# Feed-forward stage of a decoder layer: merged operations on pairs, norms ahead of expert products, and the leftover weight summed on ScalarE

## The chip, the cores and the metric

The kernel runs on one core of one Trainium2 chip. The metric is device time in microseconds of one launch. TensorE (PE) multiplies matrices, VectorE (DVE) and ScalarE (ACT) work on rows of 128 partitions, GpSimd (POOL) does the same work more slowly, and SyncE (SP) issues transfers. Each engine takes its own instructions strictly in the order in which the program lists them; engines meet only at semaphores.

## The reference

The layer has three parts, each added to the residual: a bidirectional minGRU, a cross-attention over a context of 1601 rows, and a product-key feed-forward with 256 experts. The change touches only the last part:

```python
q = (hidden_states @ Wq + bq).reshape(B, S, H, QD)          # 2048 tokens, 8 heads of 64
q = (q - mean) / jnp.sqrt(var + EPS_BN) * bn_gamma + bn_beta
q0, q1 = _l2norm(q[..., :HALF]), _l2norm(q[..., HALF:])
s0 = jnp.einsum('bshq,kq->bshk', q0, k0)                    # 32 keys each
s1 = jnp.einsum('bshq,kq->bshk', q1, k1)
ts0, ti0 = jax.lax.top_k(s0, DTK)                           # the 4 best of 32, twice
...
w = jax.nn.softmax(top_s, axis=-1)                          # over the 16 pairs
eh = gelu(einsum('bshkd,bsd->bshk', expert_down[idx], hidden_states))
out = jnp.einsum('bshko,bshk->bso', expert_up[idx], eh * w)
```

The kernel never gathers. It forms, for each token and head, a dense row of 256 weights as an outer product of 8 first-key and 32 second-key factors, sums the heads, multiplies by the gelu of all 256 expert products, and multiplies by `expert_up`.

## The kernel before

Only `stage_ffn` is touched. 2048 tokens make 16 tiles of 128 (`TILES`), two tiles make a group (`PER`), so there are 8 groups. The queries lie transposed in `raw` and `qT`, in four chunks of 128 features (`QC`), so that a group is 4 chunks of 256 columns.

Preparation. `normed` applies the batch norm (scale and bias) to the queries chunk by chunk: DVE for groups 0 and 1 (L1415), POOL for 2 and 3 (L1197), ACT from 4 on (L1274). `squared` squares them into `sq` (L1281 on ACT, L1190 and L1193 on POOL). On PE `norms(n)` (L1614) sums squares by head with 16 small products, `scores(i)` (L1625) makes a tile's scores, and `expert_product(m)` (L1602), eight in all, makes 512 tokens by 128 experts into one of four banks, which ACT's `gelu(m)` empties (L1257). Banks 0 and 1 of them are later those of `sum_heads`, banks 2 and 3 those of `mix`.

The loop over tiles i, as each engine lists it:
- DVE (L1542): `scaled(i+1)` multiplies scores by the inverse norms; `largest(i, 1)` finds the 8 largest of each head's second half, and between its instructions it issues `weight_steps` of the group before (at even i): sums, reciprocals, `share`, `first` (the 8 first-key factors), then the reduction `own` (L1507) and `clamped` = 8 - own (L1511), which releases POOL by `weights_ready`. Then at some even i `squares(k)` waits for a batch of norms; then `weigh(i-4)` (L1529) waits for `sum_heads(i-4)`; then `largest(i, 0)` and `remove(i)`, which releases POOL's `selected(i)`.
- ACT (L1322): `exponentials(i+1)` waits for `scaled(i+1)`; at even i perhaps `norm_roots`; at i = 2 the gelus 4 to 7; at odd i `normed(n+3)` and `squared(n+3)`; then `read_output(i-5)`. Sqrt, Exp and Gelu lie in different tables, and a change of table is an instruction of its own.
- POOL (L1229): `selected` (writes `near`) and two `products` per tile, each an outer product over four heads (L1152). After the first one POOL adds `clamped` to a single column of `prod` (L1218), and this lets `sum_heads` go.
- PE (L1699): `scores(i+2)`, at even i `norms(n+2)`, `mix(i-5)` (L1650), `sum_heads(i-3)` (L1634), which needs both products.

`prod` has three buffers. The last two tiles, and half of tile 13, are shared between POOL and DVE (`SHARE`).

Of the kernel before, what the change touches and what calls it, by code (L numbers as in the profile page):

```python
# [11 lines left out]
P = 128  # L12
# [999 lines left out]
def stage_ffn(nc, keep, d):  # L1012
# [27 lines left out]
    with ExitStack() as ctx:  # L1040
# [27 lines left out]
        share = st.sb("share", [P, PER * HEADS, FIRSTS])  # L1068
# [15 lines left out]
        def query(c, a, e):  # L1084
            return raw[:, c, a:e] if a < SEQ else qT[:, c, a - SEQ:e - SEQ]

        def expert_bank(m):
# [17 lines left out]
        weights_ready, prod_ready, prod_done, part_pool, part_dve, weight_mm, h_ready, out_mm = (  # L1105
            st.sem(n) for n in ("weights_ready", "prod_ready", "prod_done", "part_pool", "part_dve", "weight_mm",
# [17 lines left out]
        def wait_squares(eng, n, c):  # L1124

            if n == 0 and c < ACT_CHUNKS:
                eng.wait_ge(sq_ready, c + 1)
            elif n < 2:
                eng.wait_ge(sq_pool, QC * n + c + 1 - ACT_CHUNKS)
            else:  # L1130
                eng.wait_ge(sq_ready, ACT_CHUNKS + QC * (n - 2) + c + 1)

        def wait_query(eng, n, chunks):

            if n < FIRST_POOL:
                eng.wait_ge(q_ready_dve, QC * n + chunks)
            elif n < FIRST_ACT:
                eng.wait_ge(q_ready_pool, QC * (n - FIRST_POOL) + chunks)
            else:
                eng.wait_ge(q_ready_act, QC * (n - FIRST_ACT) + chunks)  # L1140
# [16 lines left out]
        with nc.Block() as block:  # L1157
# [11 lines left out]
            def _(pool):  # L1169
# [4 lines left out]
                pool.tensor_tensor(kinv[:], k2[:], mhalf[:], ALU.pow).then_inc(kinv_ready, 1)  # L1174
                pool.memset(pair[:], 0.0).then_inc(pair_ready, 1)
# [5 lines left out]
                pool.wait_ge(const_ready, 1)  # L1181
# [4 lines left out]
                pool.wait_ge(const_ready, 5)  # L1186
# [3 lines left out]
                for c in range(ACT_CHUNKS, QC):  # L1190
                    pool.wait_ge(q_ready_dve, c - ACT_CHUNKS + 1)
                    pool.tensor_tensor(sq[:, 0, c], q0[:, c], q0[:, c], ALU.mult).then_inc(sq_pool, 1)
                for c in range(QC):  # L1193
                    pool.wait_ge(q_ready_dve, QC + QC)
                    q = query(c, COLS, 2 * COLS)
                    pool.tensor_tensor(sq[:, 1, c], q, q, ALU.mult).then_inc(sq_pool, 1)
                for n in range(FIRST_POOL, FIRST_ACT):  # L1197
                    for c in range(QC):
                        q = query(c, n * COLS, (n + 1) * COLS)
                        pool.tensor_scalar(q, q, bn[:, 0:1], bn[:, 1:2], ALU.mult, ALU.add).then_inc(q_ready_pool, 1)  # L1200
# [42 lines left out]
            def _(act):  # L1243
# [30 lines left out]
                def normed(n):  # L1274

                    for c in range(QC):
                        q = query(c, n * COLS, (n + 1) * COLS)
                        act.activation(q, q, ACT.Identity, scale=bn[:, 0:1], bias=bn[:, 1:2])\
                            .then_inc(q_ready_act, 1)

                def squared(n):  # L1281
                    if n >= 2:
                        act.wait_ge(norm_mm, n - 1)
                    else:
                        act.wait_ge(bn_ready, 1)
                    for c in range(QC if n else ACT_CHUNKS):
                        q = query(c, n * COLS, (n + 1) * COLS)
                        if n >= 1:
                            wait_query(act, n, c + 1)
                            act.activation(sq[:, n % 2, c], q, ACT.Square).then_inc(sq_ready, 1)  # L1290
                        else:
                            act.activation(sq[:, 0, c], q, ACT.Square, scale=bn[:, 0:1], bias=bn[:, 1:2])\
                                .then_inc(sq_ready, 1)
# [28 lines left out]
                for i in range(TILES):  # L1322
# [10 lines left out]
                    if t == 1 and n + 3 < GROUPS:  # L1333
                        if n + 3 >= FIRST_ACT:
                            normed(n + 3)
                        squared(n + 3)
                    if i - WEIGH - 1 >= 0:
                        read_output(i - WEIGH - 1)
                read_output(ADDED - 1)

            @block.vector
            def _(dve):
# [72 lines left out]
                def normed():  # L1415

                    for c in (*range(ACT_CHUNKS, QC), *range(ACT_CHUNKS)):
                        dve.tensor_scalar(q0[:, c], query(c, 0, COLS), bn[:, 0:1], bn[:, 1:2], ALU.mult, ALU.add)\
                            .then_inc(q_ready_dve, 1)
                    for c in range(QC):  # L1420
                        q = query(c, COLS, 2 * COLS)
                        dve.tensor_scalar(q, q, bn[:, 0:1], bn[:, 1:2], ALU.mult, ALU.add).then_inc(q_ready_dve, 1)
# [61 lines left out]
                def weight_steps(n, a=0, e=PER):  # L1484
                    h = n % 2
                    part = [P, (e - a) * HEADS, FIRSTS]
                    lists = top[:, h, a:e].rearrange("p t h k -> p (t h) k")[:, :, 0:2 * TOPK].rearrange(
                        "p h (s k) -> p h s k", s=2)
                    kept = near[:, h, a:e].rearrange("p t h k -> p (t h) k")
                    rows = slice(a * HEADS, e * HEADS)  # L1490
                    c = note(dve.tensor_reduce(total[:, rows], lists, AX.X, ALU.add))
# [6 lines left out]
                    c = note(dve.tensor_tensor(share[:, rows], kept[:, :, 0:FIRSTS], inv[:, rows, 1:2].broadcast_to(part),  # L1498
# [3 lines left out]
                    c = note(dve.tensor_tensor(first[:, h, a:e].rearrange("p t h i -> p (t h) i"), share[:, rows],  # L1502
                                               inv[:, rows, 0:1].broadcast_to(part), ALU.mult))
                    if n * PER + e > LASTS - 1:
                        need(c)
                        dve.tensor_copy(lead[:, a:e], first[:, h, a:e])
                    c = note(dve.tensor_reduce(own[:, a:e], share[:, rows].rearrange("p (t h) i -> p t (h i)", t=e - a),  # L1507
                                               AX.X, ALU.add))
                    yield
                    need(c)  # L1510
                    dve.tensor_scalar(clamped[:, h, a:e], own[:, a:e], -1.0, float(HEADS), ALU.mult, ALU.add)\  # L1511
                        .then_inc(weights_ready, 1)
                    yield
# [77 lines left out]
            def _(pe):  # L1591
# [33 lines left out]
                def scores(i):  # L1625
                    wait_query(pe, i // PER, QC)
# [7 lines left out]
                def sum_heads(i):  # L1634
# [3 lines left out]
                    if i < LASTS:  # L1638
                        pe.wait_ge(prod_done, 2 * (i + 1) - (i in SHARE))
# [10 lines left out]
                def mix(i):  # L1650
                    if i >= 2:
                        wait_output(pe, i - 2)
                    if i < ADDED:
# [31 lines left out]
                pe.wait_ge(const_ready, 5)  # L1685
# [5 lines left out]
                expert_product(4)  # L1691
# [3 lines left out]
                for m in range(EARLY_GELU + 1, ES):  # L1695
                    expert_product(m)
# [85 lines left out]
```

## Time and profile before

| | before |
|---|---|
| median of 3 runs | 433.55 us (432.21 to 433.97) |
| the profiled execution, its own time | 433.55 us |
| its span, first to last instruction | 431.8 us |
| around the span | 1.75 us |
| PE busy | 402.8 us, 93% |
| DVE busy | 307.4 us, 71% |
| ACT busy | 225.7 us, 52% |
| POOL busy | 207.7 us, 48% |
| mean granted clock of TensorE | 0.980 |

The shares are means over three unlike parts. The feed-forward runs from 306 us on, its preparation ends about 352 us and the loop over tiles fills the rest. Matmuls are pipelined, and so a row that stands for several of them is a little longer than the distance to the next row.

### The profile page before, as it was taken

To read this page: it belongs to the slowest core of one execution; us is meant where nothing else is said; L and a number is where in the kernel's file an instruction comes from. 1 tells how busy PE (TensorE), PEld (TensorE's weight loads), DVE (VectorE), ACT (ScalarE), POOL (GpSimd) and SP (SyncE) were. 2 spreads that over 40 slices of the span, in tenths; PEclk is the share of its full clock that TensorE was granted. 3 is DMA by queue.
4 is the path that set the end of the run, shared out by engine and by line. 5 is a ranking of instruction groups with operands and counts; after the bars stand their busy time and mean duration, and the time that the engine had idled before them with its cause. 6 is when DMAs were issued, how large, how long until landed. Compare 5 with 4: busy or idle time off the path is not lost. (4 is left out here: it accounts for less than half of the span.)

```text
span 431.8 us, 7774 instructions
## 1 busy us (share of the span) xinstructions
PE 402.8 (93%) x2563; PEld 368.9 (85%) x2563; DVE 307.4 (71%) x1139; ACT 225.7 (52%) x455; POOL 207.7 (48%) x203
## 2 busy tenths in 40 slices
PE   2997999987999999999999999999999979999786
PEld 2876878876899999999999999989778979999685
DVE  5899885667656575476755555565876889899995
ACT  3774646314645455555554444444557878675300
POOL 2588988941814233342333312000112668899991
PEclk9999999999999999999999999999999877999989
DMA  7800222002322223211232100000000000001011
GB/s 227 275 2 3 74 71 77 8 0 77 102 76 77 52 77 99 56 50 53 76 93 61 53 2 2 1 2 1 26 0 2 1 2 2 27 26 37 27 35 52
DMA packets 19992, 21.38 MB, mean 50 GB/s; under 512 B 3180, under 2 KB 16624, under 8 KB 19952
## 3 DMA queue, kind: packets, MB, share of 16 engines
q1 hardware_dynamic: 18832, 19.96, 15.5%
q10 hardware_dynamic: 1120, 0.92, 0.8%
q8 instruction: 21, 0.34, 0.3%
q14 instruction: 19, 0.16, 0.1%
HBM read 18.78 MB, written 2.10 MB: 48 GB/s over the span
## 5 line engine op out<-in xcount | busy, mean ns | idle before, releaser
L960 PE MATMUL att_pA<-context_cNh,att_pTh 128*128 128x256 f32 (+1 forms) x208 | 62.6, 301 | 1.1 <-DVE att_pTl L858 1.1
L961 PE MATMUL att_pA<-context_cNl,att_pTh 128*128 128x256 f32 (+1 forms) x208 | 58.3, 280 | 0.0
L962 PE MATMUL att_pA<-context_cNh,att_pTl 128*128 128x256 f32 (+1 forms) x208 | 58.1, 280 | 0.0
L1152 POOL TENSOR_TENSOR ffn_prod<-ffn_first,ffn_near 128x1024 f32<-128x1024 f32 (+1 forms) x29 | 54.6, 1882 | 7.0 <-DVE ffn_clamped L1511 6.6
L858 DVE TENSOR_TENSOR att_pTl<-att_pR,att_pTh 128x512 fp32r<-128x512 f32 x64 | 37.4, 586 | 26.7 <-ACT att_pTh L775 26.5
L877 DVE TENSOR_REDUCE att_mx<-keep_pQ 128x1 f32<-128x402 f32 x64 | 35.6, 568 | 25.5 <-PE keep_pQ L77 25.4
L765 POOL TENSOR_TENSOR context_cTl<-keep_raw,context_cTh 128x512 fp32r<-128x512 f32 (+1 forms) x24 | 23.1, 978 | 47.9 <-ACT context_cTh L789 47.9
L765 POOL TENSOR_TENSOR context_cNl<-keep_raw,context_cNh 128x512 fp32r<-128x512 f32 (+1 forms) x21 | 25.1, 1210 | 41.9 <-ACT context_cNh L789 41.9
L960 PEld LDWEIGHTS att_pA<-context_cNh,att_pTh 128*128 128x128 f32 (+1 forms) x208 | 39.1, 188 | 2.2 <-DVE att_pTl L858 1.5
L1646 PE MATMUL ffn_pT<-keep_ident,ffn_prod 128*128 128x128 f32 x256 | 34.7, 294 | 6.5 <-POOL ffn_prod L1152 3.9
L1646 PEld LDWEIGHTS ffn_pT<-keep_ident,ffn_prod 128*128 128x128 f32 x256 | 32.0, 153 | 9.4 <-DVE ffn_hT L1533 4.7
L961 PEld LDWEIGHTS att_pA<-context_cNl,att_pTh 128*128 128x128 f32 (+1 forms) x208 | 39.3, 189 | 0.0
L962 PEld LDWEIGHTS att_pA<-context_cNh,att_pTl 128*128 128x128 f32 (+1 forms) x208 | 39.1, 188 | 0.0
L775 ACT ACTIVATE att_pTh<-att_pR 128x512 fp32r<-128x512 f32 x64 | 32.4, 516 | 9.3 <-PE att_pR L992 8.5
L219 POOL TENSOR_TENSOR gru_z<-gru_z,gru_g 128x512 f32<-128x512 f32 x16 | 31.2, 1950 | 8.3 <-DVE gru_g L407 8.3
L992 PE MATMUL att_pR<-keep_ident,att_prob 128*128 128x128 f32 (+1 forms) x208 | 32.8, 272 | 0.0
L1467 DVE MAX8 ffn_top<-ffn_e 128x8 f32<-128x32 f32 x256 | 29.5, 176 | 0.3
L75 PE MATMUL gru_pP<-gru_xTh,gru_wh 128*128 128x512 f32 x62 | 26.9, 434 | 0.0
L775 ACT ACTIVATE att_vTh<-att_pR 128x256 fp32r<-128x256 f32 x16 | 6.1, 384 | 39.4 <-PE att_pR L997 39.4
L75 PE MATMUL keep_pQ<-context_cTh,keep_qT0h 128*128 128x402 f32 (+1 forms) x64 | 23.0, 359 | 3.2 <-PEq L159 1.7
L379 DVE TENSOR_TENSOR_SCAN gru_hT<-gru_c,gru_z 128x512 f32<-128x512 f32 x16 | 24.1, 1508 | 2.2 <-POOL gru_z L219 1.6
L992 PEld LDWEIGHTS att_pR<-keep_ident,att_prob 128*128 128x128 f32 (+1 forms) x208 | 24.8, 140 | 0.7
(285 smaller groups left out, 1138.7 us busy)
## 6 DMA issues: line engine op xcount, KB each, us to landing
keep_raw<-in_ctxT SPq DMA_DIRECT2D x24, 256.0 KB, 2.6
keep_raw<-in_ctx SPq DMA_DIRECT2D x24, 256.0 KB, 2.7
out<-keep_x SPq DMA_DIRECT2D x16, 128.0 KB, 1.7
keep_x<-in_x SPq DMA_DIRECT2D x3, 512.0 KB, 10.0
gru_wout<-in_W_out SPq DMA_DIRECT2D x1, 512.0 KB, 8.4
keep_raw<-in_fWq SPq DMA_DIRECT2D x2, 256.0 KB
keep_raw<-in_ctxT SPq DMA_DIRECT2D x8, 32.5 KB, 3.6
keep_raw<-in_ctx SPq DMA_DIRECT2D x4, 65.0 KB
```

What stands on the lines that cost most here:

```text
L75: pe.matmul(out, lh, rh, start=(i == 0), stop=False)
L219: pool.tensor_tensor(z[:, n % ZB], z[:, n % ZB], g[:, u % 2], ALU.mult).then_inc(zg_ready, 1)
L765: pool.tensor_tensor(lo, raw(i % RAW), hi.bitcast(F32), ALU.subtract).then_inc(piece_lo, 1)
L775: act.activation(to, bank, ACT.Copy).then_inc(bank_high, 1)
L858: dve.tensor_tensor(to, bank, half(it, 0, n)[0].bitcast(F32), ALU.subtract).then_inc(bank_free, 1)
L877: last = dve.tensor_reduce(mx[:, h, j:j + 1], pS[:, j, 0:min(SPANS[j][1], CTX) - SPANS[j][0]], AX.X, ALU.max)
L960: pe.matmul(pA[:, 0:D], l[0], r[0], start=(kt == 0), stop=False)
L961: pe.matmul(pA[:, 0:D], l[0], r[1], start=False, stop=False)
L962: last = pe.matmul(pA[:, 0:D], l[1], r[0], start=False, stop=(kt == CT - 1))
L992: last = pe.transpose(bank[0:rows, m * P:(m + 1) * P], prob[:, a % 2, kt * P:kt * P + rows], ident[:])
L1152: return eng.tensor_tensor(prod[:, i % PB, a:b].rearrange("p h (i j) -> p h i j", j=KEYS), (factor if factor is not None else first[:, n % ...
L1646: last = pe.matmul(pW[:, i % 2, c * P:(c + 1) * P], prod[:, i % PB, h, c * P:(c + 1) * P], ident[:], start=(h == 0), stop=(h == HEADS - 1) ...
```

## The change

Six edits, all in `stage_ffn`:
1. `normed` and `squared` take a whole group in one instruction (128x1024), or a pair of chunks (128x512) for group 0 and for POOL's squares. Their semaphores count groups.
2. On PE `norms(1)` moves ahead of expert product 4 and `norms(2)` ahead of product 5; `norms(3)` goes ahead of `scores(4)`; products 6 and 7 move into the loop, behind `scores(5)` at i = 3.
3. The first `sum_heads` waits for six gelus where it waited for eight; the first `mix` waits for eight.
4. DVE's `own` and `clamped` and POOL's addition go, for tiles 0 to 13. In their place ACT gets `leftover(i)`: a Copy with scale -1 over 65 numbers, with its sum taken (64 shares and a constant -8), then an addition of the sum to the one column of `prod`. For the last group DVE keeps its own way.
5. `weights_ready` is set by `first`. `sum_heads(i)` waits for `last_ready` of ACT and for the second product.
6. `leftover(i-3)` stands in ACT's loop at i, behind `exponentials(i+1)`, `normed` and `squared`.

```diff
-                        pool.wait_ge(prod_ready, i + 1)
-                        last = prod[:, i % PB, 0, EXPERTS - 1:EXPERTS]
-                        pool.tensor_tensor(last, last, clamped[:, n % 2, t:t + 1], ALU.add).then_inc(prod_done, 1)
...
-                    for c in range(QC):
-                        q = query(c, n * COLS, (n + 1) * COLS)
-                        act.activation(q, q, ACT.Identity, scale=bn[:, 0:1], bias=bn[:, 1:2])\
-                            .then_inc(q_ready_act, 1)
+                    act.activation(queries(n), queries(n), ACT.Identity, scale=bn[:, 0:1], bias=bn[:, 1:2])\
+                        .then_inc(q_ready_act, 1)
...
+                        wait_query(act, n)
+                        act.activation(sq[:, n % 2], queries(n), ACT.Square).then_inc(sq_ready, 1)
...
+                def leftover(i):
+
+                    n, t = i // PER, i % PER
+                    act.wait_ge(weights_ready, weights_at(i))
+                    act.wait_ge(const_ready, 6)
+                    rest = clamped[:, n % 2, t:t + 1]
+                    act.activation(spare[:], share[:, n % 2, t], ACT.Copy, scale=-1.0, accum_out=rest).then_inc(own_ready, 1)
+                    act.wait_ge(prod_ready, i + 1)
+                    act.wait_ge(own_ready, i + 1)
+                    last = prod[:, i % PB, 0, EXPERTS - 1:EXPERTS]
+                    act.activation(last, last, ACT.Identity, bias=rest).then_inc(last_ready, 1)
...
                         if n + 3 >= FIRST_ACT:
                             normed(n + 3)
                         squared(n + 3)
+                    if i >= SUM:
+                        leftover(i - SUM)
                     if i - WEIGH - 1 >= 0:
                         read_output(i - WEIGH - 1)
+                leftover(LASTS - 1)
                 read_output(ADDED - 1)
...
                     if i < LASTS:
-                        pe.wait_ge(prod_done, 2 * (i + 1) - (i in SHARE))
+                        pe.wait_ge(last_ready, i + 1)
+                        if i not in SHARE:
+                            pe.wait_ge(prod_done, i + 1)
...
-                expert_product(4)
                 norms(1)
                 scores(2)
                 scores(3)
-                for m in range(EARLY_GELU + 1, ES):
-                    expert_product(m)
+                expert_product(EARLY_GELU)
                 norms(2)
+                expert_product(EARLY_GELU + 1)
                 pe.wait_ge(ld_up, 16)
                 for i in range(TILES):
                     n, t = i // PER, i % PER
+                    if i == PER:
+                        norms(n + 2)
                     if 4 <= i + 2 < TILES:
                         scores(i + 2)
+                    if i == PER + 1:
+                        for m in range(EARLY_GELU + 2, ES):
+                            expert_product(m)
...
                         if i == SUM:
-                            pe.wait_ge(gelu_ready, ES)
+                            pe.wait_ge(gelu_ready, EARLY_GELU + 2)
                         sum_heads(i - SUM)
```

## Rows read from the trace of the kernel before

**Rows 1.** Busy time in stretches: us, PE, PEld, DVE, ACT, POOL, granted clock, DMA.
```profile
350.00:360.00 10.00, 7.18 (x45) 6.72 (x44) 9.02 (x69) 9.13 (x20) 5.43 (x6) 0.66 0.01 2
360.00:370.00 10.00, 10.00 (x72) 9.80 (x72) 8.68 (x74) 7.51 (x20) 9.65 (x9) 0.83 0.05 14
370.00:380.00 10.00, 10.00 (x81) 9.54 (x80) 8.69 (x72) 6.69 (x17) 7.85 (x9) 1.00 0.04 14
```

**Rows 2.** The chain in order of time, one turn of PE's loop: start, us, what.
```profile
368.62 0.89 PE keep_pQ L1631 x8
369.52 1.68 PE ffn_pK L1622 x16
371.20 0.54 PE keep_pQ L1654 x2
...
372.60 1.75 PE ffn_pT L1646 x16
```

**Rows 3.** Timeline of POOL: start, us, line, operation, tiles, [idle before <-releaser].
```profile
372.13 1.91 POOL L1152 TENSOR_TENSOR ffn_prod<-ffn_first,ffn_near 128x1024 f32<-128x1024 f32 x1 [2.00 <-DVE ffn_clamped L1511]
...
386.76 1.91 POOL L1152 TENSOR_TENSOR ffn_prod<-ffn_first,ffn_near 128x1024 f32<-128x1024 f32 x1
388.75 0.19 POOL L1218 TENSOR_TENSOR ffn_prod<-ffn_prod,ffn_clamped 128x1 f32<-128x1 f32 x1
388.89 0.86 POOL L1205 TENSOR_TENSOR ffn_near<-ffn_e,ffn_picked 128x320 f32<-128x320 f32 x1
```

**Rows 4.** Timeline of ACT between i = 2 and i = 4.
```profile
353.45 1.09 ACT L1260 ACTIVATE ffn_gT<-keep_pQ 128x512 f32<-128x512 f32 x2
354.56 1.28 ACT L1305 ACT_TABLE_LOAD   x1
355.85 0.42 ACT L1305 ACTIVATE ffn_e<-ffn_s 128x256 f32<-128x256 f32 x1
...
356.79 2.06 ACT L1278 ACTIVATE ffn_qT<-ffn_qT,ffn_bn 128x256 f32<-128x256 f32 x4
358.76 1.32 ACT L1290 ACTIVATE ffn_sq<-ffn_qT 128x256 f32<-128x256 f32 x4
```

**Rows 5.** Timeline of PE where the preparation ends and summing begins.
```profile
350.47 1.60 PE L1631 MATMUL keep_pQ<-ffn_keyT,ffn_qT 128*128 128x128 f32 x8
354.60 3.51 PE L1646 MATMUL ffn_pT<-keep_ident,ffn_prod 128*128 128x128 f32 x16 [2.52 <-ACT ffn_gT L1260]
```

**Rows 6.** Timeline of DVE: `weigh(0)`, `scaled(6)`, `squares(3)`, `scaled(8)`, `squares(4)`, the tail's first product.
```profile
359.69 0.41 DVE L1533 TENSOR_TENSOR ffn_hT<-ffn_pT,ffn_gT 128x256 f32<-128x256 f32 x1
...
362.32 0.68 DVE L1459 TENSOR_TENSOR ffn_s<-keep_pQ,ffn_ninv 128x512 f32<-128x512 f32 x1
...
371.24 0.23 DVE L1429 TENSOR_SCALAR ffn_n<-ffn_pK 128x64 f32<-128x64 f32 x1 [1.58 <-PE ffn_pK L1622]
...
374.81 0.68 DVE L1459 TENSOR_TENSOR ffn_s<-keep_pQ,ffn_ninv 128x512 f32<-128x512 f32 x1
...
390.85 0.21 DVE L1429 TENSOR_SCALAR ffn_n<-ffn_pK 128x64 f32<-128x64 f32 x1
...
416.75 1.21 DVE L1152 TENSOR_TENSOR ffn_prod<-ffn_pB,ffn_near 128x1024 f32<-128x1024 f32 x1
```

**Rows 7.** Groups of ACT by form: tiles, count | busy us, mean ns | idle before.
```profile
L810 ACT ACTIVATE att_prob<-keep_pQ,att_nmax 128x1206 f32<-128x1206 f32 x16 | 20.3, 1270 | 5.7 <-DVE att_nmax L884 4.4
...
L1278 ACT ACTIVATE ffn_qT<-ffn_qT,ffn_bn 128x256 f32<-128x256 f32 x16 | 8.2, 586 | 0.0
L1290 ACT ACTIVATE ffn_sq<-ffn_qT 128x256 f32<-128x256 f32 x24 | 7.9, 401 | 0.0
...
L813 ACT ACTIVATION_READ_ACCUMULATOR att_prob<-keep_pQ,att_nmax 128x1 f32 x16 | 3.2, 200 | 0.0
...
L1298 ACT ACTIVATE ffn_nroot<-ffn_n 128x32 f32<-128x32 f32 x2 | 0.5, 230 | 1.1 <-DVE ffn_n L1429 1.1
```

**Rows 8.** The two groups of DVE that go, by form.
```profile
L1507 DVE TENSOR_REDUCE ffn_own<-ffn_share 128x2 f32<-128x128 f32 x6 | 1.7, 277 | 0.0
...
L1511 DVE TENSOR_SCALAR ffn_clamped<-ffn_own 128x2 f32<-128x2 f32 x6 | 1.2, 194 | 0.0
```

More of the change, by code:

```diff
@@ L1085, in query, with queries @@
             return raw[:, c, a:e] if a < SEQ else qT[:, c, a - SEQ:e - SEQ]
+        def queries(n, a=0, e=QC):
+            lo, hi = n * COLS, (n + 1) * COLS
+            return raw[:, a:e, lo:hi] if lo < SEQ else qT[:, a:e, lo - SEQ:hi - SEQ]
         def expert_bank(m):
@@ L1283, in squared @@
                         act.wait_ge(norm_mm, n - 1)
+                        wait_query(act, n)
+                        act.activation(sq[:, n % 2], queries(n), ACT.Square).then_inc(sq_ready, 1)
                     else:
                         act.wait_ge(bn_ready, 1)
[L1286 to L1293, printed above, removed]
+                        act.activation(sq[:, 0, 0:ACT_CHUNKS], queries(0, 0, ACT_CHUNKS), ACT.Square, scale=bn[:, 0:1],
+                                       bias=bn[:, 1:2]).then_inc(sq_ready, 1)
                 def norm_roots(k):
@@ L1415, in normed @@
                 def normed():
[L1417 to L1422, printed above, removed]
+                    for c in (ACT_CHUNKS, 0):
+                        dve.tensor_scalar(q0[:, c:c + ACT_CHUNKS], queries(0, c, c + ACT_CHUNKS), bn[:, 0:1], bn[:, 1:2],
+                                          ALU.mult, ALU.add).then_inc(q_ready_dve, 1)
+                    dve.tensor_scalar(queries(1), queries(1), bn[:, 0:1], bn[:, 1:2], ALU.mult, ALU.add)\
+                        .then_inc(q_ready_dve, 1)
                 def squares(k):
@@ L1497, in weight_steps @@
                     dve.wait_ge(near_ready, n * PER + e)
-                    c = note(dve.tensor_tensor(share[:, rows], kept[:, :, 0:FIRSTS], inv[:, rows, 1:2].broadcast_to(part),
+                    if n >= 2:
+                        dve.wait_ge(own_ready, (n - 1) * PER)
+                    c = note(dve.tensor_tensor(shares, near[:, h, a:e, :, 0:FIRSTS], by[:, :, :, 1:2].broadcast_to(part),
                                                ALU.mult))
@@ L1501, in weight_steps @@
                     need(c)
-                    c = note(dve.tensor_tensor(first[:, h, a:e].rearrange("p t h i -> p (t h) i"), share[:, rows],
-                                               inv[:, rows, 0:1].broadcast_to(part), ALU.mult))
-                    if n * PER + e > LASTS - 1:
+                    scaled_shares = dve.tensor_tensor(first[:, h, a:e], shares, by[:, :, :, 0:1].broadcast_to(part), ALU.mult)
+                    if n < GROUPS - 1:
+                        scaled_shares.then_inc(weights_ready, 1)
+                        if n * PER + e == LASTS:
+                            dve.wait_ge(weights_ready, weights_at(LASTS - 1))
+                            dve.tensor_copy(lead[:, a:e], first[:, h, a:e])
+                        yield
+                    else:
+                        c = note(scaled_shares)
                         need(c)
                         dve.tensor_copy(lead[:, a:e], first[:, h, a:e])
[L1507 to L1513, printed above, removed]
+                        c = note(dve.tensor_reduce(own[:, a:e], share[:, h, a:e, 0:HEADS * FIRSTS], AX.X, ALU.add))
+                        yield
+                        need(c)
+                        dve.tensor_scalar(clamped[:, h, a:e], own[:, a:e], -1.0, float(HEADS), ALU.mult, ALU.add)\
+                            .then_inc(weights_ready, 1)
+                        yield
                 def shared_products(i):
@@ L1700, in _ @@
                     n, t = i // PER, i % PER
+                    if i == PER:
+                        norms(n + 2)
                     if 4 <= i + 2 < TILES:
                         scores(i + 2)
-                    if t == 0 and 3 <= n + 2 < GROUPS:
+                    if i == PER + 1:
+                        for m in range(EARLY_GELU + 2, ES):
+                            expert_product(m)
+                    if t == 0 and 4 <= n + 2 < GROUPS:
                         norms(n + 2)
```

56 lines of the change are left out of this document (30 added, 26 removed).

## The prediction

> **What bounds the kernel now.** I read the busy time by stretch first, then each engine's timeline of the loop, then the chain. Only the feed-forward after 330 us changes. In 350 to 360 us PE is busy 7.18 us of 10 at a granted clock of 0.66, and in 370 to 380 us it is busy all the time at 1.00 [rows 1]. So PE lacks work just where the loop begins, and from 360 to about 390 us it has none of its time to give away: a turn of two tiles needs scores (0.89), norms (1.68), mix (371.20 to 372.60: 1.40), the summing of heads (1.75), then scores, mix without the norms' delay (I take 1.3) and summing again: 0.89 + 1.68 + 1.40 + 1.75 + 0.89 + 1.3 + 1.75 = 9.7 us [rows 2]. POOL is the other full engine, with four products of 1.91, two selections of 0.86 and two small additions in a turn: about 9.8 us [rows 3]. DVE stands where it waits for PE's norms, 1.58 us before 371.24 [rows 6]. Once the last norms are through (390.85), DVE and POOL alone carry the loop to 416.75, where the tail begins [rows 6].
>
> **The change, part by part.**
>
> *POOL's addition goes.* From the start of the product at 386.76 to the selection at 388.89 are 2.13 us, 0.22 more than the product itself; fourteen of these are 3.1 us of POOL. The 2.00 us that POOL waited before 372.13 for `clamped` goes too, since `first` is made before the wait for norms [rows 3]. Neither reaches the end if something else than POOL sets the turn, and PE's 9.7 us stands right below POOL's 9.8. I count them at zero between 350 and 390 us. If POOL alone counted they would be worth up to 5 us.
>
> *DVE loses `own` and `clamped`,* 0.277 + 0.194 us busy, so at most 0.47 and at least, overlapped, about 0.25 per group [rows 8]. I take 0.4. It matters after 390 us, in two groups and the rest of a third: 0.9 us. DVE's waits for POOL's `near` go as well once POOL has 0.5 us less to do in a turn. They show in the stretch to 416.75 as about 0.5 us, an estimate between 0 and 1.
>
> *Merged operations on ACT.* Four in-place norms take 2.06 us and four squares 1.32, together 356.79 to 360.08, 3.3 us [rows 4]. No row has 1024 elements. A line from 256 elements (586 ns) to 1206 (1270 ns) gives 1.14 us for the norm, and from 401 ns 1.10 for the square [rows 7]. The square now waits for all of the norm, which costs the overlap of the two: together 2.3 us, bounds 2.0 and 2.6. So an odd i is 1.0 us shorter on ACT. The merged operations on DVE and POOL lie at 331 to 341 us beside PE's work, which is the same set in another order. One of them could hold back the first norms by some tenths, since PE now waits for a pair of chunks where it waited for one. I take 0 and keep 0 to 0.5.
>
> By the Trainium skill, ScalarE: Activation LUTs, What ACT_TABLE_LOAD costs, an ACTIVATE takes 186 ns plus 0.833 ns per element and 93 ns for each pointer operand; this would make 1.23 + 1.04 us, the same 2.3. The trace agrees at 256 elements (586 and 401 ns).
>
> *The leftover on ACT.* A Copy with its sum is at least the smallest ACTIVATE, 230 ns, and a read of the accumulator, 200 ns; the addition is another 230 ns or more, and it waits for the first to land [rows 7]. With 0.1 for that wait: 0.8 us, bounds 0.66 and 1.1. It is three instructions of 0.66 us for DVE's pair and POOL's addition, but the size isn't what counts. ACT is not full (7 to 9 us of 10) [rows 1]. What counts is its place: `sum_heads(i-3)` now waits for ACT to be through `exponentials(i+1)`, and at odd i through `normed` and `squared` as well. Before, it waited only for POOL's products. Behind that wait PE has the next scores and the next norms; and DVE's `weigh(i-4)`, with `remove` and the next `scaled` behind it, waits for PE.
>
> The same page, Rules for kernel authors, says to use VectorE and not ScalarE for add and mul; the rows here, 0.47 us of DVE against 0.66 to 0.8 of ACT, agree in direction.
>
> *The new order on PE.* Up to the loop PE does the same products as before, with expert products 6 and 7 last. So product 7 ends where `scores(5)` ended, 352.1 us [rows 5], and PE gives ACT the last of the eight banks at about 352.2. DVE gets its norms sooner: before, norms 3 came right ahead of `scores(5)` and ended at 350.5 [rows 5], now products 6 and 7 and one tile's scores (together about 3.5 us) lie behind them, and they end near 347. DVE, busy by itself until 349, is then some 1.7 us ahead by i = 4.
>
> **The sum,** in the time of the profiled span:
> 1. Gelu 7 ends at 352.2 + 0.6 = 352.8 (before 354.54). Then the table, 1.28, the three exponentials, 0.94 (355.85 to 356.79), norm and square 2.3, leftover 0.8: `sum_heads(0)` starts at 358.1 [rows 4]. Before it started at 354.60 [rows 5]. PE stands idle for 6 us where it stood 2.5. The six gelus of edit 3 don't help, for ACT has the table, `exponentials(4)` and group 4 between them and the leftover.
> 2. PE starts from idle. At 354.60 the sixteen transposes took 3.51 us, against 1.75 in a full turn [rows 2, 5], with a granted clock of 0.66 over the stretch [rows 1], that is the lower level, 1.2 GHz, for most of the time PE was busy. I take 3.5 again: `weigh(0)` at 361.7 instead of 359.69 [rows 6]. DVE's lead of 1.7 is lost and 2.0 us more.
> 3. From `weigh(0)` to `scaled(6)` were 2.63 us [rows 6], now 2.5, so 364.2; scaled 0.7, exponentials 0.95, norm and square 2.3, leftover 0.8: `sum_heads(2)` at 369.0. PE by itself would be there at 361.6 + 0.9 + 1.7 + 1.75 + 0.9 + 1.3 = 368.1 at full clock, 369.8 if the second sum is slow too. I take 369.0. Plus 1.75 + 0.9 + 1.7: norms 5 end at 373.3, 2.1 later than before.
> 4. `squares(3)` waits for them. From it to `scaled(8)` were 3.57 us, now 3.4 without `clamped` [rows 6]: 376.7. Plus 0.7 + 0.95 + 2.3 + 0.8: `sum_heads(4)` at 381.5. PE by itself would be there at 373.3 + 1.4 + 1.75 + 0.9 + 1.3 = 378.7. It idles 2.8 us.
> 5. From there PE's own work holds: 9.7 to `sum_heads(6)`, 1.75, scores 0.9 and norms 1.7 bring norms 7 to 395.5. `squares(4)` was at 390.85 [rows 6]: +4.7. If the idle 2.8 us bring the low clock, up to 1.7 more. I add 0.3, since a sum may miss it altogether.
> 6. From `squares(4)` to 416.75 were 25.9 us [rows 6]. Less 0.9 and 0.5: 24.5. Net 5.0 - 1.4 = +3.6, less 0.1 for rounding in the steps. POOL, with 9.1 us in a turn, follows. The tail has the same work and moves as a whole.
>
> So +3.5 us. The profiled execution took 433.55 us, 1.75 around its span, and the median of the runs is the same: **437.0 us**.
>
> **The rivals.**
> *Faster: the leftover is in time.* If ACT reached it before PE had nothing else to do, DVE's 1.7 us of lead and the 1.4 us of step 6 would both stay: 433.55 - 3.1 = 430.4. It decides at `sum_heads(0)`: an ACT that gets there by 356 us doesn't delay `weigh(0)`. For it: ACT has idle time in every stretch and DVE and POOL really lose work. Against: the idle time lies before the exponentials, and four instructions stand between these and the leftover by the program's order. 0.13.
> *Same: only the first wait counts.* If the second idle time (step 4) isn't there, because the norms or ACT's work come sooner than my steps, `sum_heads(4)` starts at 378.7, norms 7 end at 392.7, and +1.8 less 1.4 gives 434.0. What speaks for it is that steps 3 and 4 add five durations each of which may be 0.2 too long. 0.22.
> *Slower still: the clock.* PE idles 6 us and 2.8 us, and each idle time can be followed by a stretch at the lower level, as before 360 and again up to 370 (0.83) [rows 1]. Two sums more at 3.5 instead of 1.75 us in the part that PE sets: 437.0 + 2 to 3 = 439.5. 0.19. The Trainium skill, TensorE: Matmul & The Clock Gate, Part 1, says that the clock is released by activity and falls back when PE is idle; the 3.51 us sum after 2.5 us of idle time agrees.
> *The forecast,* one late start and one more idle time at about this size: 0.46.
>
> **How the numbers follow.** The forecast gives 437.0 with its own range of 435.5 to 438.5. The measurement can tell about 0.5%, 2.2 us, from no change, so slower means above 435.7. Slower gets the forecast nearly whole, 0.44, and the clock's 0.19, so 0.63; same gets the middle rival and the edge of the forecast, 0.24; faster 0.13. The range has to take in the middle rival and most of the clock: 431.6 to 440.0, which leaves out most of the faster case and little above.
>
> **What would show it.** In the profile after: expert product 7 ends near 352; ACT's addition for tile 0 comes last before the first transposes, near 358, and PE's idle time before them names ACT, some 6 us; the first sum takes about 3.5 us; DVE waits about 3.8 us before `weigh(0)` for PE; PE waits again for ACT before `sum_heads(4)`, about 2.8 us; `squares(4)` near 395.8; POOL's wait for `clamped` is gone and POOL waits for `picked` instead, so that its busy time is smaller and its idle time larger. The merged norm is 1.1 to 1.25 us and the square 1.0 to 1.1. I am wrong if the first transposes start before 356.5, if PE is again busy throughout 370 to 390 us, or if a leftover costs 0.4 us rather than 0.8.

## The result and the profile after

The changed kernel took **441.81 us** (median of 4 runs, 439.65 to 443.57) against 433.65 us of the kernel before, a ratio of 1.0196 with a 95% interval of 1.0152 to 1.0240. A second set of nine runs, side by side with the experiments, gave 440.67 us and 1.0137 (1.0091 to 1.0183). So it is slower, as forecast, but by 7 to 8 us and not by 3.5, and outside the range of 431.6 to 440.0. The ratios leave out runs more than 1.5% above the fastest of their kernel (three of e_noleft, one each of e_first and e_reorder, and one execution of the kernel before at 1023.64 us), and the medians have them in, so that e_noleft's 434.48 below would be 432.71 without them. The profiled execution of the changed kernel is its fastest of the four:

| | before | after |
|---|---|---|
| profiled execution | 433.55 us | 439.65 us |
| span | 431.8 us | 437.8 us |
| PE busy | 402.8 us | 401.2 us |
| DVE busy | 307.4 us | 304.6 us |
| ACT busy | 225.7 us | 228.2 us |
| POOL busy | 207.7 us | 202.9 us |
| mean granted clock of TensorE | 0.980 | 0.984 |

DVE and POOL have lost the work that the change takes from them (2.8 and 4.8 us), and yet the end comes 6 us later. Busy time in stretches of the kernel after, columns as in [rows 1]:

```profile
350.00:360.00 10.00, 3.60 (x17) 2.97 (x16) 7.33 (x53) 9.28 (x20) 7.14 (x5) 0.72 0.00 0
360.00:370.00 10.00, 9.11 (x72) 8.63 (x71) 7.99 (x66) 4.69 (x12) 6.03 (x6) 0.93 0.00 2
370.00:380.00 10.00, 9.01 (x70) 8.16 (x68) 7.17 (x61) 6.27 (x14) 7.98 (x5) 1.00 0.08 28
380.00:390.00 10.00, 8.22 (x54) 8.05 (x55) 7.12 (x58) 3.92 (x14) 8.31 (x6) 0.83 0.04 14
```

PE was busy 7.18, 10.00 and 10.00 us in the first three of these [rows 1] and is now busy 3.60, 9.11 and 9.01. All the other engines have room, over these stretches as a whole. PE's timeline, where it was [rows 5], says what it waits for; only rows of summing, and what follows the fifth, are shown:

```profile
351.35 0.39 PE L77 MATMUL keep_pQ<-ffn_xT3h,ffn_dnl 128*128 128x512 f32 x1
358.14 3.48 PE L1666 MATMUL ffn_pT<-keep_ident,ffn_prod 128*128 128x128 f32 x16 [6.40 <-issue]
...
364.06 1.95 PE L1666 MATMUL ffn_pT<-keep_ident,ffn_prod 128*128 128x128 f32 x16
...
369.09 1.94 PE L1666 MATMUL ffn_pT<-keep_ident,ffn_prod 128*128 128x128 f32 x16 [0.89 <-issue]
...
381.77 3.60 PE L1666 MATMUL ffn_pT<-keep_ident,ffn_prod 128*128 128x128 f32 x16 [2.77 <-issue]
...
393.69 1.94 PE L1666 MATMUL ffn_pT<-keep_ident,ffn_prod 128*128 128x128 f32 x16 [0.41 <-issue]
...
396.37 1.85 PE L1640 MATMUL ffn_pK<-ffn_group_of,ffn_sq 128*128 128x4 f32 x16
```

The releaser is given as "issue": the profile doesn't name what ended the wait. ACT's timeline, against [rows 4], does. The last line ends at 358.05 and the first sum begins at 358.14:

```profile
354.11 0.42 ACT L1301 ACTIVATE ffn_e<-ffn_s 128x256 f32<-128x256 f32 x1
...
355.04 1.23 ACT L1278 ACTIVATE ffn_qT<-ffn_qT,ffn_bn 128x1024 f32<-128x1024 f32 x1
356.36 1.06 ACT L1285 ACTIVATE ffn_sq<-ffn_qT 128x1024 f32<-128x1024 f32 x1
357.32 0.24 ACT L1317 ACTIVATE ffn_spare<-ffn_share 128x65 f32<-128x65 f32 x1
357.47 0.19 ACT L1317 ACTIVATION_READ_ACCUMULATOR ffn_spare<-ffn_share 128x1 f32 x1
357.75 0.30 ACT L1321 ACTIVATE ffn_prod<-ffn_prod,ffn_clamped 128x1 f32<-128x1 f32 x1
```

DVE, with the rows that answer to [rows 6]: `weigh(0)`, `squares(3)`, `squares(4)` and the tail's first product. And POOL, against [rows 3]: no wait for `clamped`, a wait for `picked` instead.

```profile
361.66 0.42 DVE L1551 TENSOR_TENSOR ffn_hT<-ffn_pT,ffn_gT 128x256 f32<-128x256 f32 x1 [4.00 <-PE ffn_pT L1666]
...
373.64 0.23 DVE L1439 TENSOR_SCALAR ffn_n<-ffn_pK 128x64 f32<-128x64 f32 x1 [2.80 <-PE ffn_pK L1640]
...
398.25 0.22 DVE L1439 TENSOR_SCALAR ffn_n<-ffn_pK 128x64 f32<-128x64 f32 x1 [2.31 <-PE ffn_pK L1640]
...
422.80 1.21 DVE L1157 TENSOR_TENSOR ffn_prod<-ffn_pB,ffn_near 128x1024 f32<-128x1024 f32 x1
```

```profile
364.50 0.86 POOL L1210 TENSOR_TENSOR ffn_near<-ffn_e,ffn_picked 128x320 f32<-128x320 f32 x1 [2.42 <-DVE ffn_picked L1490]
```

**Two sums that sort the time.** From stretches of 1 us between 330 and 400 us I took, for every kernel, PE's idle time and what the low clock cost it: busy time × (1 − granted clock), since at 1.2 of 2.4 GHz half of a busy microsecond is lost. Two such stretches of the kernel after, in the fifth sum and behind it:

```profile
382.00:383.00 1.00, 1.00 (x6) 1.00 (x6) 1.00 (x9) 1.00 (x5) 1.00 (x1) 0.50 0.17 60
...
386.00:387.00 1.00, 1.00 (x12) 1.00 (x10) 0.96 (x12) 0.00 (x0) 1.00 (x1) 1.00 0.00 0
```

| kernel | leftover on ACT | PE's order | median, us (runs) | ratio to before (95%) | profiled span | PE idle | lost to the clock |
|---|---|---|---|---|---|---|---|
| before | no | old | 433.55 (3) | | 431.8 | 3.0 | 5.6 |
| after | last | new | 441.81 (4) | 1.0196 (1.0152–1.0240) | 437.8 | 10.6 | 4.9 |
| after_again | last | new | 440.67 (9) | 1.0137 (1.0091–1.0183) | 439.4 | 9.8 | 7.4 |
| e_onlyleft | last | old | 443.60 (6) | 1.0258 (1.0224–1.0292) | 441.9 | 15.7 | 4.9 |
| e_mid | middle | new | 433.79 (11) | 1.0022 (0.9992–1.0052) | 429.3 | 6.0 | 1.7 |
| e_first | first | new | 433.01 (12) | 0.9998 (0.9958–1.0037) | 427.8 | 5.4 | 1.7 |
| e_first_old | first | old | 431.89 (11) | 0.9993 (0.9955–1.0032) | 430.0 | 3.4 | 5.3 |
| e_noleft | no | new | 434.48 (12) | 0.9997 (0.9955–1.0039) | 436.1 | 2.9 | 8.5 |
| e_merge | no | old | 432.42 (12) | 0.9979 (0.9950–1.0007) | 429.5 | 4.8 | 3.3 |
| e_reorder | no | new | 432.01 (11) | 0.9999 (0.9961–1.0036) | 429.9 | 5.6 | 1.7 |

Apart from before, all but e_onlyleft and e_reorder have the merged operations. For the kernel after, the account closes: 7.6 us more idle time, 0.6 us less lost to the clock, and 1.0 us less in the part that POOL sets (below) make 6.0 us, and the spans differ by 6.0. For the other kernels the same account misses the difference of the spans by 0 to 1.8 us, so it sorts the time and doesn't prove where it went.

### The profile page after: what moved, and what is told of

It reads as the page before. It is cut to its first block and busy times, and to the rows that moved or that the text cites. A ratio compares the mean times of both kernels' runs of the same rounds, so it can differ in the third digit from the quotient of the medians.

```text
span 437.8 us, 7772 instructions
## 1 busy us (share of the span) xinstructions
PE 401.2 (92%) x2563; PEld 366.8 (84%) x2563; DVE 304.6 (70%) x1118; ACT 228.2 (52%) x466; POOL 202.9 (46%) x181
## 5 line engine op out<-in xcount | busy, mean ns | idle before, releaser
L1666 PEld LDWEIGHTS ffn_pT<-keep_ident,ffn_prod 128*128 128x128 f32 x256 | 31.1, 152 | 17.9 <-issue 12.9
```

The costliest lines, as they stand in the source:

```text
L1666: last = pe.matmul(pW[:, i % 2, c * P:(c + 1) * P], prod[:, i % PB, h, c * P:(c + 1) * P], ident[:], start=(h == 0), stop=(h == HEADS - 1) ...
```

## The experiments

**1. The change without the leftover (e_noleft).** DVE and POOL do their old work again; merged operations and PE's new order stay.

```diff
-                    if i >= SUM:
-                        leftover(i - SUM)
...
+                        pool.tensor_tensor(last, last, clamped[:, n % 2, t:t + 1], ALU.add).then_inc(prod_done, 1)
```

> The changed kernel with one part undone: DVE makes own and clamped again and POOL adds the column; ACT has no leftover. Merges and the new order on PE stay. Theory (the leftover's place in ACT's queue makes PE late, at the first sum of heads and again at the fifth): both idle stretches of PE go, the first sum starts right behind the sixth gelu, near 352 us, instead of 358.1, squares(4) comes before 391, and the time is 430 to 433. Rival A (the new order on PE or the merges cost the time): still above 438. Rival B (half and half): 434 to 438.

434.48 us, 0.9997 (0.9955 to 1.0039): by the ratio the loss is gone, though the median of all twelve runs lies in rival B's band. So the leftover carries all of it, within the 0.4% of the interval, and the merged operations and the order together give nothing that can be told from none. Its profiled execution was its slowest, 437.91 us, with 2.9 us of idle time and 8.5 us lost to the clock, 5.1 of them ahead of 350 us. In it the first sum began at 356.43 and `squares(4)` at 395.03, later than the theory had them (352, 391), with no leftover in the kernel: so much can the clock alone do.

**2. The leftover alone (e_onlyleft).** The kernel before, with the leftover on ACT.

> The kernel before with the leftover alone: on ACT behind exponentials, norm and square; four-chunk norms and squares and the old order on PE stay. Theory (place): ACT gets to the first leftover at 354.6 + 1.3 + 0.9 + 3.3 = 360.1, so the first sum starts near 361 where it started at 354.6, later still than in the changed kernel: 443 to 448. Rival (the new order and the merges are the cause): 433 to 436.

443.60 us, 1.0258 (1.0224 to 1.0292), 10 to 11 us slower than before and 2 to 3 us slower than the whole change. PE's timeline of this kernel; the first sum waits 9.19 us, the fifth 3.66:

```profile
358.39 3.64 PE L1670 MATMUL ffn_pT<-keep_ident,ffn_prod 128*128 128x128 f32 x16 [9.19 <-issue]
...
383.89 3.65 PE L1670 MATMUL ffn_pT<-keep_ident,ffn_prod 128*128 128x128 f32 x16 [3.66 <-issue]
```

The first sum begins within 0.25 us of where it does in the kernel after: ACT's queue sets it, whenever PE is through. The theory had it near 361, reckoned from gelus that ended at 354.54 as before; here they ended at 352.13. With norm and square still in four pieces each, 3.3 us instead of 2.4 stand ahead of each odd tile's leftover. So the other edits don't pay by themselves, but beside the leftover on ACT they do, most likely by the 0.9 us that merging takes out of ACT's queue; which of them does it was not tried.

**3. The leftover at the head of ACT's loop (e_first).** One move in the kernel after:

```diff
+                    if i >= SUM:
+                        leftover(i - SUM)
                     if 2 <= i + 1 < TILES:
                         exponentials(i + 1)
...
-                    if i >= SUM:
-                        leftover(i - SUM)
```

> The changed kernel with leftover(i-3) at the head of ACT's loop, ahead of exponentials(i+1), where it stood behind exponentials, norm and square. Same instructions, same waits. Theory (place, not cost): the first sum starts near 353.6, there is no idle time before the fifth, and the time is 430 to 433, like without the leftover or a little better since DVE and POOL keep their savings. Rival (the three ACT instructions cost it, 0.8 us each time): above 438. Second rival: the leftover now holds back the exponentials wherever POOL's product is late, above all for tiles 9 to 12: 434 to 437.

433.01 us, 0.9998 (0.9958 to 1.0037). The first sum begins at 352.34 instead of 358.14. The profile names a gelu for its wait, but the six gelus that it needs had ended at 350.64; ACT's addition, behind gelus 6 and 7, came last, at 352.23:

```profile
349.56 1.08 ACT L1262 ACTIVATE ffn_gT<-ffn_pT 128x512 f32<-128x512 f32 x2
350.53 1.09 ACT L1262 ACTIVATE ffn_gT<-keep_pQ 128x512 f32<-128x512 f32 x2
...
351.94 0.29 ACT L1321 ACTIVATE ffn_prod<-ffn_prod,ffn_clamped 128x1 f32<-128x1 f32 x1
```

```profile
352.34 1.94 PE L1666 MATMUL ffn_pT<-keep_ident,ffn_prod 128*128 128x128 f32 x16 [2.19 <-ACT ffn_gT L1262]
```

So even here the leftover sets the first start, but 1.6 us behind the gelus instead of 6.3 (in the kernel after the six gelus ended at 351.81), and before the fifth sum there is no idle time. The work is the same as in the kernel after, to the instruction. Only its place in a queue differs, and that is worth 6 to 9 us (by the ratios 1.4 to 2.0%, by the medians 7.7 and 8.8 us).

**4. The leftover between exponentials and norm (e_mid).** It still stands behind the table load and the exponentials, but no longer behind norm and square.

```diff
+                    if i >= SUM:
+                        leftover(i - SUM)
                     if t == 1 and n + 3 < GROUPS:
```

> The changed kernel whole, with ScalarE's sum of the leftover moved behind the exponentials of the next tile and ahead of the merged norm and square. The first leftover then stands behind the table load and the exponentials (end near 355.5) instead of behind 1.2 us of norm and 1.1 us of square as well. Theory (the place in ScalarE's queue is what the wait costs): the first sum of heads starts near 356, TensorE idle there 4 us where the changed kernel showed 6.4, and by the fifth sum, where no table stands, the idle time falls from 2.8 us to at most 1; the time comes out between the kernel with the leftover first (433.0) and the changed one (440.7), near 435.5, and nearer to the first if the clock at the fifth sum stays at full speed. Rival A (a leftover on ScalarE costs wherever it stands unless it stands first, since the exponentials wait for DVE): 438 or more. Rival B (only the norm and the square in front mattered): 433 to 434.

433.79 us, 1.0022 (0.9992 to 1.0052), a figure of rival B. The theory had the first sum right (355.17 for 356, 4.54 us of idle time for 4) and the fifth (0.47 us for at most 1), but put the price of the first start too high:

```profile
355.17 3.09 PE L1666 MATMUL ffn_pT<-keep_ident,ffn_prod 128*128 128x128 f32 x16 [4.54 <-issue]
...
375.55 1.94 PE L1666 MATMUL ffn_pT<-keep_ident,ffn_prod 128*128 128x128 f32 x16 [0.47 <-issue]
```

So of the three things in front of the leftover (table and exponentials, norm, square) the last two, 2.3 us of ACT, make nearly all of the 7 us between this kernel and the changed one. They work twice. They hold up the first sum by 3.0 us (the preparation's end, 1.1 us earlier here, is part of that), and they open the second gap: `leftover(4)` ends 0.4 us after PE wants it here (375.44 for 375.08) and 2.7 us after in the kernel after. The low clock that comes behind the second gap there doesn't come here.

**5. The kernel after, again (after_again).**

> The changed kernel once more, unaltered, beside the others of this call, to see how its runs spread and on what. Theory (late additions plus the clock after them): median 440 to 443, and the runs order themselves by the mean granted clock, 439.7 at 0.984 as before and 443 to 444 at 0.973 to 0.976: each 0.004 of mean clock, 1.7 us of lost cycles, is 1 to 1.7 us of time. Rival (the spread has nothing to do with the clock): no order.

440.67 us. The nine runs sort by their mean granted clock, as the theory had it, and reach lower than it had: 436.63 to 437.14 at 0.992, 439.67 and 440.67 at 0.984, 441.29 and 441.34 at 0.98, 442.68 and 443.04 at 0.976. Its profiled execution (441.29) has nearly the same two gaps as the first (5.98 and 2.75 us), and 2.5 us more lost to the clock, 1.5 of them ahead of 350 us, before the change does anything to PE's gaps:

```profile
340.00:350.00 10.00, 9.90 (x53) 9.01 (x52) 9.77 (x81) 7.62 (x13) 5.82 (x5) 0.68 0.01 2
```

The kernel after had 1.00 here in its first profile.

**6. Products in the gaps (e_warm, e_warm2).** To see what the clock costs, PE multiplies the identity by itself, for nobody, ahead of sums 1 and 5: 48 and 22 products, then half as many.

```diff
+                        for _ in range({SUM: 48, SUM + 4: 22}.get(i, 0)):
+                            pe.matmul(pW[:, 0, DC * P:(DC + 1) * P], ident[:], ident[:], start=True, stop=True)
```

> The changed kernel, with 48 products of 128 columns that nobody reads put ahead of PE's wait at the first sum of heads and 22 ahead of the fifth, each group shorter than the idle time it fills (5.3 of 6.4 us, 2.4 of 2.8 us). The waits stay. Theory (what the forecast missed is the lower clock after the two idle stretches): sums 1 and 5 take 1.75 us instead of 3.5 and 3.6, squares(4) comes 3.5 us sooner, the time is 437 to 439 and the runs spread less than the 4 us of the changed kernel. Rival (the clock is beside the point, the late addition sets all): 441 to 442.

444.86 us, 1.0276 (1.0235 to 1.0316). A product took 0.229 us, twice what I had counted, so that the 48 stood in the way: 10.98 us of them where the gap was 6.4. As a measure of the gain this failed. But the clock stayed at 1.00 in every stretch from 330 to 400 us, and both sums took 1.91 us instead of 3.5 and 3.6; `squares(4)` came no sooner for it, at 400.04.

> The changed kernel with idle products ahead of the waits again, now sized by what they take: one such 128-column product in this type took 0.229 us (96 matmuls for 48 products, 10.98 us), twice what I had counted, and so 48 and 22 of them overran the idle times. Now 24 (5.5 of 6.4 us) and 11 (2.5 of 2.8). Theory (the clock after the idle times is what the forecast missed): mean clock at or near 1.0, first and fifth sum of heads 1.75 us, time 437 to 439. Rival (the clock is beside the point): 441 to 443.

439.14 us, 1.0090 (1.0050 to 1.0131), against 440.67 and 1.0137 without them, measured side by side; the two intervals overlap. In its profile the sums take 1.94 us each. It lost 5.1 us to the clock all the same, all of them between 343 and 354 us, ahead of the first unread product:

```profile
354.84 5.52 PE L1737 MATMUL ffn_pT<-keep_ident 128*128 128x128 f32 x48
360.98 1.94 PE L1666 MATMUL ffn_pT<-keep_ident,ffn_prod 128*128 128x128 f32 x16 [0.62 <-issue]
...
380.14 2.62 PE L1737 MATMUL ffn_pT<-keep_ident 128*128 128x128 f32 x22
383.06 1.94 PE L1666 MATMUL ffn_pT<-keep_ident,ffn_prod 128*128 128x128 f32 x16 [0.30 <-issue]
```

That the slow sums are the clock is shown; that this makes some 1.5 us of the 7 is likely. The remainder is the gaps themselves: two runs of e_warm2 with a mean clock of 1.000 took 434.96 and 435.61 us, where the three of e_first at 0.996 took 429.45 to 430.56, so that the gaps cost some 5 us (an estimate from these five runs).

**7. Merging alone and the order alone (e_merge, e_reorder, e_first_old).**

> The kernel before with the merged operations alone: old order on PE, no leftover on ACT. Theory: norm and square on ACT are 1.0 us shorter at odd i, but nobody waits for them in the kernel before but norms 4 (0.3 us), so 432.5 to 434, no change. Rival (merging costs, since squares and norms now come in one piece and norms wait for the whole of it): 435 to 437. Other rival (ACT gives what it saves to the gelus and the exponentials): 430 to 432.

> The kernel before with TensorE's new order around the first products alone: no merged operations and no leftover on ScalarE. Theory A (the order is neutral): within 1 us of the kernel before, 432.5 to 434.5. Theory B (the new order lets the clock fall between 340 and 350 in some runs): the median 1 to 2 us above the kernel before, with a wider spread, the fastest runs level with it. Rival C (norms and scores of later groups come earlier and so POOL's and DVE's work too, which ends the waits of TensorE in front of the fourth and later norms): 1 to 2 us faster.

> Merged operations and the leftover on ScalarE at the head of its loop, with TensorE's order as in the kernel before. Theory A (the new order of TensorE adds nothing once the leftover is early): the same as the kernel with the leftover first and the new order, 433.0 within 1 us. Theory B (the new order bunches the narrow products of norms and scores ahead of the wait for the gelus, and the clock sometimes falls there, between 340 and 350 us): 1 to 2 us faster than that one, 431 to 432, and no profile of it has a granted clock under 0.9 between 340 and 350. In either case TensorE's idle time ahead of the first sum of heads is 2 to 3 us and is ended by the gelu.

432.42, 432.01 and 431.89 us, with ratios within 0.25% of 1 (0.9979, 0.9999, 0.9993) and each with 1 in its interval. Neither edit gains or costs anything that can be measured. e_merge fits its theory to 0.1 us. e_reorder fits theory A by its ratio (0.9999), though its median is 0.5 us under the band. e_first_old has the figure of theory B, but its ratio, 0.9993, can't be told from the 0.9998 of e_first. On the mechanism of B, that the new order lets the clock fall between 340 and 350 us, the profiles lean one way: 4 of the 9 kernels with the new order that were profiled have 0.65 to 0.69 there, and none of the 5 with the old. The spread of the runs leans the same way (7.5, 7.1 and 7.5 us in e_noleft, e_reorder and e_first, 2.8 and 5.2 in e_merge and e_first_old), but e_mid, with the new order, spreads by 3.9 only, and 27 runs of the kernel before by 5.7. The old order has its low stretches elsewhere: in 3 of its 5 profiles the clock fell at 334 us. The medians show no price; this stays open.

**8. The best version (e_first_warm, e_old_warm).** e_first with 5 unread products before the first sum and 7 before norms 4; and e_first_old with 5 before the first sum.

> The kernel with the leftover at the head of ACT's loop, with 5 idle products ahead of the first sum of heads (1.1 of 2.2 us of idle time) and 7 ahead of norms 4 (1.6 of 1.8 us). Theory (the clock makes the spread of 429.5 to 436.9 there): the slow second sum, 3.36 us, becomes 1.75 and the median goes from 433.0 to 429 to 431, a version ahead of both kernels. Rival (the idle products fall behind what the waits allow, and delay): 433 to 435.

431.28 us, 0.9948 (0.9916 to 0.9979), just above the theory's band. In its profiled execution (433.75, one of its slower ones) the second sum still took 2.91 us; the clock fell at 363.6, behind norms 4.

> The kernel with merged operations, the leftover at the head of ScalarE's loop and TensorE's order as before, and in addition five products of the identity with itself, which nobody reads, in TensorE's idle time ahead of the first sum of heads (behind the fifth gelu). Without them that sum started at 355.50 after 3.06 us of idle time and took 3.65 us. Theory (the clock after idle time is what the idle time costs beyond its length): the first sum takes under 2.5 us, the time is 1 to 1.5 us less than without them, 430.5 to 431, and the ratio to the kernel before under 0.997. Rival (such products don't lift the clock, they only stand in the way; or the gain in the earlier kernel with them was drift between calls): the sum takes 3.5 us as before, and the time is 432 or more with a ratio of 0.999 or above.

429.80 us, 0.9960 (0.9925 to 0.9996). The time came out as in the theory and a little below its band, the reason didn't show: in the profiled execution the first sum took 3.49 us all the same. That execution (432.33) is again one of the slower of its kernel; the fastest, at 0.988 to 0.992, have no profile.

```profile
352.90 1.38 PE L1731 MATMUL ffn_pT<-keep_ident 128*128 128x128 f32 x10 [1.51 <-ACT ffn_gT L1262]
355.03 3.49 PE L1666 MATMUL ffn_pT<-keep_ident,ffn_prod 128*128 128x128 f32 x16 [0.75 <-ACT ffn_gT L1262]
```

The five products ran at full clock, it fell at 354.8, between them and the sum, and PE had stood still for 2.3 of the 3.6 us before the sum. So a few products in a gap don't hold the clock every time, and the gain of these two kernels, 0.4 to 0.5%, is shown as a time and not explained. Their intervals overlap that of e_first_old. Both beat the kernel before, by just about what can be measured.

## Why the forecast had the sign and not the size

The step that failed is 5: it put the low clock behind the second gap at 0.3 us, and the fifth sum alone took 1.7 us more than at full clock. With it the profiled execution came 2.6 us above the forecast; the other 2.2 us of the miss lie between that execution and the median.

**Right: the mechanism and steps 1 to 4.** The start of the fifth sum, the end of a long chain of added durations, came 0.3 us off. That is in part luck: the profile of after had the same low stretch ahead of 350 us as the one of before, and in after_again the first sum began at 359.66.

| step | forecast | trace |
|---|---|---|
| product 7 ends | 352.1 | 351.74 |
| idle time before the first sum | 6 | 6.40 |
| first sum starts, takes | 358.1, 3.5 | 358.14, 3.48 |
| `weigh(0)` | 361.7 | 361.66 |
| third sum | 369.0 | 369.09 |
| norms 5 end (`squares(3)`) | 373.3 | 373.64 |
| fifth sum; idle time before it | 381.5; 2.8 | 381.77; 2.77 |
| `squares(4)` | 395.8 | 398.25 |
| from there to the tail | 24.5 | 24.55 |

The operations came as bounded: merged norm 1.23 and square 1.06 us, 2.38 from the start of one to the end of the other (2.3), the leftover 0.73 (0.8) from its start to the addition's end. The Trainium skill (ScalarE: Activation LUTs, What ACT_TABLE_LOAD costs) gives 1.23 and 1.04; the trace agrees, and the line through [rows 7] gave 1.14 for the norm.

Step 6 holds as well, and better than the medians let one see. From the tenth sum to the sixteenth, where POOL sets the pace, are 22.97 us (408.58 to 431.55), and 22.97, 22.97 and 22.96 in e_mid, e_first and e_onlyleft; 23.94 before, and 23.96, 23.96 and 23.95 in e_noleft, e_merge and e_reorder. So taking the work from DVE and POOL is worth 1.0 us there, whatever else is changed.

**Wrong: step 5, the clock after the second gap.** "I add 0.3, since a sum may miss it altogether." From the fifth sum to `squares(4)` I had 14.05 us and those 0.3; the trace has 16.5. Of the 2.4 us over 14.05, 1.7 are the fifth sum (3.42 us until the scores follow it, for 1.75), 0.4 one more gap, before the seventh sum, where ACT's leftover is late once more, and 0.3 small ones behind `mix` and norms 7. The rival "slower still: the clock" had this mechanism and this place, with 2 to 3 us, and I gave it 0.19.

The same miss can be told from the other side. The kernel before has a stretch of low clock under its second sum, too:

```profile
361.08 3.54 PE L1646 MATMUL ffn_pT<-keep_ident,ffn_prod 128*128 128x128 f32 x16
```

That cost it 1.6 us. Step 3 let it vanish, by taking the rows behind at nearly full clock. The trace of after bears that out (1.95 us), but it was booked as a gain without one of like size in a new place. In these two profiles the stretches moved: 5.6 us lost to the clock before, 4.9 after, in both cases in three stretches between 330 and 400 us, of 1.6 to 2.2 us each. It is no rule, for over all profiles the loss goes from 0 (e_warm) to 8.5 us.

One reading of the prediction doesn't hold. Step 2 and the rival of the clock took the slow first sum before for a consequence of its 2.5 us of idle time. But the clock had fallen at 351.0, behind norms 3, while PE was busy and a microsecond ahead of the idle time:

```profile
351.00:352.00 1.00, 1.00 (x6) 0.78 (x4) 1.00 (x14) 0.98 (x2) 0.00 (x0) 0.50 0.00 0
```

The 3.5 us taken from it came true (3.48); in the kernel after the clock fell within the idle time, at 354.5.

**Wrong too: one execution taken for the median.** The profiled one is the fastest of four, and 439.65 would have lain inside the range. The nine later runs reach from 436.6 to 443.0 us with one program. The forecast stood where the runs at a mean clock of 0.992 came out, 436.6 to 437.1 us; none of these was profiled, so that whether they miss the low clock behind the second gap wasn't seen. I had before me three runs within 1.8 us and made the range from mechanisms alone; 27 later runs of the kernel before cover 5.7 us. Ahead of 350 us alone the fourteen profiles lost to the clock 0 (six of them), 1.7 (before, after, e_first_old, e_old_warm), 3.2 to 3.5 (after_again, e_warm2, e_first_warm) and 5.1 us (e_noleft).

**The rivals.** "The leftover is in time" was priced at 430.4, deciding at 356 us on ACT. e_first and e_mid meet that condition, with first sums at 352.34 and 355.17, and their medians don't come to it (433.0 and 433.8); their fastest runs (429.5 and 431.4) are near it, but so are those of the kernel before (430.1 to 430.6). "Only the first wait counts" is out: the second gap came at its forecast size.

## What to carry to other kernels

Before an operation is put on an engine with room, look not at the room but at what stands ahead of it in that engine's queue when its consumer is ready: here 0.7 us of work on an engine that is half idle cost 7 us, and nothing that can be told from none (1.0022 and 0.9998) once moved ahead of 2.3 us of work that was needed later. A gap opened in a PE-bound stretch should be priced with a spell at the lower clock behind it (both profiles of the changed kernel have one behind both of their long gaps), and a spell that the old trace shows should not be booked as a gain. Where a few microseconds decide, one profile is one draw: ask first how far the runs of one program spread with the clock.

## What the hardware showed that I had not expected

- The granted clock falls not only after gaps. In the kernel after it fell at 334 us, with PE busy 9.88 us of the 10 around it; just ahead of the fall stood norms 0, 16 products with 4 columns each. In the kernel before all three falls between 330 and 400 us (333.9, 351.0, 361.2) lie within about half a microsecond behind norms, with PE busy.

```profile
330.00:340.00 10.00, 9.88 (x66) 9.29 (x66) 7.63 (x37) 8.03 (x13) 5.68 (x6) 0.83 0.01 2
```

  In e_first it fell at 358.5 us, within norms 4 and behind a gap of 1.84 us. The Trainium skill (TensorE: Matmul & The Clock Gate, Part 1) ties the lower level to idle time; the traces have it behind narrow products without a gap as well. Whether the narrow products are the cause was not tried.
- When it falls differs from run to run of one program: between 340 and 350 us, with the same products, 1.00 in one execution of the kernel after and 0.68 in the next.
- A product of 128 columns of float32 takes 0.229 us (96 records in 10.98 us for 48 products), where a transpose of the same size takes 0.11 (16 in 1.75 us).
- A Copy of 65 numbers with its sum issues a second instruction, the read of the accumulator, at 0.19 us, and the addition that needs it starts 0.28 us after that one's start: 0.73 us for 66 numbers.
